# Two more source tiles in float32r, low parts by an accumulating transfer, and a ring of five logit buffers

## What is computed

```python
def gat_layer(x, W, att_src, att_dst, bias, src, dst, heads, out_ch, concat):
    n = x.shape[0]
    h = (x @ W.T).reshape(n, heads, out_ch)
    a_src = jnp.einsum('nhc,hc->nh', h, att_src)
    a_dst = jnp.einsum('nhc,hc->nh', h, att_dst)
    e = jax.nn.leaky_relu(a_src[src] + a_dst[dst], 0.2)
    m = jax.ops.segment_max(e, dst, num_segments=n)
    ex = jnp.exp(e - m[dst])
    denom = jax.ops.segment_sum(ex, dst, num_segments=n)
    alpha = ex / (denom[dst] + 1e-16)
    out = jax.ops.segment_sum(alpha[:, :, None] * h[src], dst, num_segments=n)
    return out.reshape(n, heads * out_ch) + bias        # concat
```

## Time and profile before

| | |
|---|---|
| median of three runs | 714.68 us |
| profiled execution, its own time | 713.25 us |
| its span | 711.4 us |
| TensorE (PE) busy | 701.1 us (99%) |
| TensorE's weight loads (PEld) | 657.9 us (92%) |
| VectorE (DVE) busy | 529.0 us (74%) |
| ScalarE (ACT) busy | 420.0 us (59%) |
| GpSimd (POOL) busy | 114.1 us (16%) |
| granted clock | 1.00 |

### The profile page before, as it was taken

One profiled execution on the slowest core, in us unless ns is written; L12 is line 12 of the kernel. 1 busy time (PEld: TensorE's weight loads), 2 busy tenths in 40 slices (PEclk: granted clock), 3 DMA queues, 4 the chain that ended last, 5 costly groups with the idle time before them and its releaser, 6 DMA issues.

```text
span 711.4 us, 13502 instructions
## 1 busy us (share of the span) xinstructions
PE 701.1 (99%) x4670; PEld 657.9 (92%) x4670; DVE 529.0 (74%) x878; ACT 420.0 (59%) x863; POOL 114.1 (16%) x95
## 2 busy tenths in 40 slices
PE   8899999999999999999999999999999999999997
PEld 6699999889899999999999999999999899999997
DVE  5999888698899999999999664445568752737232
ACT  4665584388688888888888754454443333522202
POOL 2559421000000000000000000000223331222202
PEclk9999999999999999999999999999999999999999
DMA  8727888645314131322310443201881734315102
GB/s 279 223 68 195 262 244 232 174 140 163 95 40 114 31 102 55 94 67 64 102 32 22 109 111 67 62 0 36 247 282 49 222 91 189 100 58 177 44 23 67
DMA packets 53362, 84.10 MB, mean 118 GB/s; under 512 B 15081, under 2 KB 36399, under 8 KB 53312
## 3 DMA queue, kind: packets, MB, share of 16 engines
q1 hardware_dynamic: 47628, 65.69, 32.6%
q10 hardware_dynamic: 4500, 13.82, 6.0%
q0 software_dynamic: 1184, 3.92, 1.9%
HBM read 68.09 MB, written 15.33 MB: 117 GB/s over the span
## 4 chain that ended last, share of the span: by engine, by line
PE 91%; DMA 4%; DVE 3%; issue 0%; POOL 0%; ACT 0%; ACTq 0%; SPq 0%; DVEq 0%
PE bank L1426 22%; PE bank L1571 13%; PE bank L1402 12%; PE bank L1498 12%; PE bank L1298 11%; PE bank L1675 4%; DMA w1n_sb<-in_W 3%; PE bank L1647 3%; PE bank L1213 3%; PE bank L1552 2%; PE bank L1701 1%; DVE x2f L2312 1%; PE bank L1215 1%; PE bank L1228 1%; PE bank L1732 1%; DVE fc_lo L2279 1%
## 5 line engine op out<-in xcount | busy, mean ns | idle before, releaser
L1426 PE MATMUL bank<-PT,h1s 125*128 125x250 f32 x730 | 161.0, 374 | 0.0
L1426 PEld LDWEIGHTS bank<-PT,h1s 125*128 125x128 f32 x730 | 135.3, 190 | 14.4
L2078 DVE SCALAR_TENSOR_TENSOR L<-asb,nadh 125x1250 f32<-125x1250 f32 x80 | 117.9, 1515 | 1.9 <-PE bank L1402 0.9
L2087 DVE CUSTOM_DVE_ANT_0 L<-L,LC 125x1250 f32<-125x1250 f32 x80 | 113.4, 1454 | 0.6 <-DMA LC<-log_count_scratch 0.4
L914 ACT ACTIVATE L<-L,nm 125x1250 f32<-125x1250 f32 x80 | 108.4, 1384 | 2.7 <-DVE nm L2087 1.9
L932 ACT COPY PT<-bank 125x500 f32<-125x500 f32 x165 | 87.4, 613 | 35.9 <-PE bank L1402 35.9
L1402 PE MATMUL bank<-ident,L 125*125 125x125 f32 x800 | 94.2, 273 | 0.0
L1402 PEld LDWEIGHTS bank<-ident,L 125*125 125x125 f32 x800 | 91.2, 189 | 0.9 <-issue 0.4
L1884 DVE TENSOR_TENSOR hotr<-iota,r 125x1500 f16<-125x1500 f16 x50 | 46.5, 931 | 7.8 <-PE bank L1215 4.2
L743 POOL MEMSET pick<- 128x90 f32 x1 | 0.2, 168 | 267.2 <-ACT hT L965 267.2
L1571 PE MATMUL bank<-h_hi,PT_hi 125*125 125x384 f32 x200 | 41.5, 350 | 0.0
(11 more groups left out here) (285 smaller groups left out, 1353.9 us busy)
## 6 DMA issues: line engine op xcount, KB each, us to landing
asb<-src_logit_rows SPq DMA_DIRECT2D x28, 312.5 KB, 3.9
atom_w<-in_atom_inT SPq DMA_DIRECT2D x5, 1152.0 KB, 12.5
atom_w<-in_atom_outT SPq DMA_DIRECT2D x5, 1152.0 KB, 9.4
log_count_scratch<-LCw SPq DMA_DIRECT2D x10, 546.9 KB
LC<-log_count_scratch SPq DMA_DIRECT2D x10, 546.9 KB
LCt<-log_count_scratch SPq DMA_DIRECT2D x10, 546.9 KB
h_scratch<-h1st ACTq DMA_DIRECT2D x10, 448.0 KB
rdT<-reciprocal_scratch SPq DMA_DIRECT2D x8, 500.0 KB, 4.6
```

The lines of the kernel that those rows point to most:

```text
L1426: mm = pe.matmul(sums, h1s[q][:, s, :], PT[p][:, s, :], start=(s == 0), stop=(plain and s == NT - 1))
L2078: dve.scalar_tensor_tensor(L[r][:, :], asb[q][0:NP, 1, :], nadh[q][:, t:t + 1], asb[q][0:NP, 0, :], ALU.add, ALU.max).then_inc(stt_done, 1)
L2087: dve.tensor_tensor_reduce(out=L[r][:, :], in0=L[r][:, :], in1=LC[:, t, :], scale=-1.0, scalar=-FLOOR, op0=ALU.add, op1=ALU.min, accum_out ...
```

## The change

Source tiles 0, 1 and 2 are split now, not tile 2 alone. Tile 0 is split as before, with VectorE's subtraction. For tiles 1 and 2 ScalarE writes a float32r high part and a raw copy with opposite signs, and the low parts are their sum, made by two transfers on POOL's queue: one copies the two raw tiles to PT_sum, the next adds the two high ones onto it. Signs are mended by features with the sign changed (`h1p_neg`). The features' low parts and the changed signs are POOL's now, three instructions a head. L has five buffers, and VectorE does in a step the second tile of its group and the first of the next (`blocks`). ScalarE does the first tile's exponential ahead of the evacuation, the second's behind it. To make room, the reciprocals' rows share one buffer, rdA lies where asb[1] does, and W2 is one transfer. asb is loaded in three pieces, and W2's products move to steps 3 and 4 of head 0.

```diff
-QUARTERS = 4
-PART = 2
+TURNED_BANKS = NG * NG * H
+PIECES = [0, 834, 1667, 2500]
+RING = 5
+PART = 0
...
+def blocks(k, first):
+
+    if first and k < 3:
+        return [(2 * k, 2 * k + 1)]
+    if first and k == 3:
+        return [(6,), (7, 8)]
+    if k == 0:
+        return [(0,), (1, 2)]
+    if k == 2 * NG - 1:
+        return [(2 * k + 1,)]
+    return [(2 * k + 1, 2 * k + 2)]
...
+            sp.wait_ge(wattp, 3)
+            sp.dma_start(w2_sb[:, :, 0:D], W2T.rearrange("(k p) n -> p k n", p=128)).then_inc(w2_in, 16)
...
+                if t < 2:
+                    sp.wait_ge(stt_done, NT * H)
...
+            def lower_by_sum(hh, kk):
+
+                n, p = 2 * NG * hh + kk, kk % 2
+                pool.wait_ge(tb_evac, NG * n + 2)
+                alone(pool)
+                pool.dma_start(PT_sum[p][:, :, :].bitcast(F32), PT[p][:, 1:3, :]).then_inc(raw_moved, 16)
+                pool.wait_ge(raw_moved, 16 * n + (16 - 16 * NG))
+                alone(pool)
+                pool.dma_start(PT_sum[p][:, :, :].bitcast(F32), PT_hi[p][:, 1:3, :].bitcast(F32), accum_op=ALU.add
+                               ).then_inc(lower_moved[p], 16)
+                if kk % NG == 0:
+                    q = kk // NG % 2
+                    pool.wait_ge(features_high, 2 * hh + kk // NG)
+                    alone(pool)
+                    pool.tensor_tensor(h1p_lo[q][:, 0:2, :], h1s[q][:, 0:2, :], h1p_hi[q][:, 0:2, :].bitcast(F32),
+                                       ALU.subtract)
+                    pool.tensor_tensor(h1p_lo[q][:, 2, :], h1p_hi[q][:, 2, :].bitcast(F32), h1s[q][:, 2, :],
+                                       ALU.subtract)
+                    pool.tensor_scalar(h1p_neg[q][:, :, :], h1p_hi[q][:, 1:3, :].bitcast(F32), -1.0, None, ALU.mult
+                                       ).then_inc(features_lower, 1)
+
+            for kk in range(NG, 2 * NG):
+                lower_by_sum(0, kk)
+            with pool.Fori(1, H // 2) as hh:
+                for kk in range(2 * NG):
+                    lower_by_sum(hh, kk)
...
                     if b == PART // 2 and not (first and k - lag < NG):
-                        act.copy(PT_hi[(k - lag) % 2][:, :], turned[0:NP, 0:GW])
-                        act.copy(PT[(k - lag) % 2][:, PART + 1, :], turned[0:NP, GW:2 * GW]).then_inc(tb_evac, 1)
+                        act.copy(PT_hi[(k - lag) % 2][:, 0:2, :],
+                                 turned[0:NP, 0:2 * GW].rearrange("p (s n) -> p s n", s=2))
+                        act.activation(PT[(k - lag) % 2][:, 1, :], turned[0:NP, GW:2 * GW], ACT.Copy, scale=-1.0
+                                       ).then_inc(tb_evac, 1)
+                    elif b == 1 and not (first and k - lag < NG):
+                        act.copy(PT[(k - lag) % 2][:, 2:4, :],
+                                 turned[0:NP, 0:2 * GW].rearrange("p (s n) -> p s n", s=2))
+                        act.activation(PT_hi[(k - lag) % 2][:, 2, :], turned[0:NP, 0:GW], ACT.Copy, scale=-1.0
+                                       ).then_inc(tb_evac, 1)
...
-                    if plain or s != PART:
-                        mm = pe.matmul(sums, h1s[q][:, s, :], PT[p][:, s, :], start=(s == 0), stop=(plain and s == NT - 1))
+                    if plain or s > 2:
+                        mm = pe.matmul(sums, h1s[q][:, s, :], PT[p][:, s, :], start=(s == (0 if plain else 3)), stop=(plain and s == NT - 1))
                 if not plain:
                     if g == 0:
                         pe.wait_ge(features_lower, h)
                     pe.wait_ge(lower_done, n + (1 - NG))
-                    pe.matmul(sums, h1p[q][:, 0, :], PT_hi[p][:, :], start=False, stop=False)
-                    pe.matmul(sums, h1p[q][:, 1, :], PT_hi[p][:, :], start=False, stop=False)
-                    mm = pe.matmul(sums, h1p[q][:, 0, :], PT_lo[p][:, :], start=False, stop=True)
+                    for s in range(3):
+                        high = h1p_neg[q][:, 1, :] if s == 2 else h1p_hi[q][:, s, :]
+                        pe.matmul(sums, high, PT_hi[p][:, s, :], start=False, stop=False)
+                        pe.matmul(sums, h1p_lo[q][:, s, :], PT_hi[p][:, s, :], start=False, stop=False)
+                    pe.matmul(sums, h1p_hi[q][:, 0, :], PT_lo[p][:, :], start=False, stop=False)
+                    pe.wait_ge(lower_moved[p], 16 * NG * hh + 16 * ((k - lag) // 2 - (NG // 2 - p)))
+                    pe.matmul(sums, h1p_neg[q][:, 0, :], PT_sum[p][:, 0, :], start=False, stop=False)
+                    mm = pe.matmul(sums, h1p_hi[q][:, 2, :], PT_sum[p][:, 1, :], start=False, stop=True)
...
-                if k == 6:
+                if k == 3:
...
+                for tiles in blocks(k, first):
+                    for s in tiles:
...
+                        if not (first and s < RING):
+                            dve.wait_ge(tb_full, NG * (2 * NG * hh + ((s - RING) // 2 + 1)))
```

More of the change, by code:

```diff
@@ L428, in gnn_ffn_kernel @@
         w1_hi_done, w1_lo_done, xT_lo_done = sem("w1_hi_done"), sem("w1_lo_done"), sem("xT_lo_done")
+        raw_moved, lower_moved = sem("raw_moved"), [sem(f"lower_moved{p}") for p in range(2)]
         features_high, features_lower, lower_done = sem("features_high"), sem("features_lower"), sem("lower_done")
@@ L905, in _, with exp @@
                     act.activation(early_exp[:, :], tiny[:, :], ACT.Exp)
-            def exp(hh, k, first=False, last=False):
+            def exp(hh, k, j, first=False, last=False):
                 if last:
@@ L949, in rows_out_of @@
                 act.wait_ge(rden_turned, m + 1)
-                to = rlast[:, ds(hh if k else hh + -1, 1), 0:NP] if (t0, t1) == (LATE, NT) else None
-                if to is None:
-                    to = rrow[t0:t1, ds(h, 1), 0:NP]
-                act.copy(to.rearrange("t a n -> t (a n)"), bank[4][0:t1 - t0, 0:NP]).then_inc(rden_rows, 1)
+                freed(act, rden_stored, 16 * m)
+                act.copy(rrow[0:t1 - t0, 0:NP], bank[4][0:t1 - t0, 0:NP]).then_inc(rden_rows, 1)
             def sums_out(hh, k, first=False, last=False):
@@ L1444, in turn_reciprocals @@
                     pe.wait_ge(rden_rows, m)
-                if first and k == NG + LATE // 2:
+                if first and k == NG:
                     pe.wait_ge(watt_done, 6)
@@ L2072, in logits @@
-                for j in range(2):
-                    r, t = (2 * k + j) % 4, 2 * g + j
-                    if not (first and k < 2):
-                        dve.wait_ge(tb_full, NG * n + -NG)
-                    elif k == 1:
-                        dve.wait_ge(lc_stored[0], TWO * NG)
-                    dve.scalar_tensor_tensor(L[r][:, :], asb[q][0:NP, 1, :], nadh[q][:, t:t + 1], asb[q][0:NP, 0, :],
-                                             ALU.add, ALU.max).then_inc(stt_done, 1)
-                reciprocals(hh, k, first=first)
```

167 lines of the change are left out of this document (87 added, 80 removed).

## The result

The changed kernel takes 732.62 us (median of four runs, 731.37 to 738.54) against 714.13 us for the kernel before (713.36 to 715.59, four runs): a ratio of 1.027, with a 95% interval of 1.025 to 1.030. It is **slower by 18.5 us**, where 710.5 was forecast, 4 us faster. The profiled execution has a span of 729.5 us against 711.4. One execution of a later run, e17_one_tile, took 998 us at a granted clock of 0.655 and is left out of its median.

A forecast was written before the change was run, and what follows sets the result against it. TensorE was taken as the bound, VectorE 3% behind. Terms -5.5 + 0.3 + 1.0 = -4.2 against the runs' median of 714.68 gave 710.5 us; range 708.0 to 733.0.

The forecast's parts named there:

- Step 1: TensorE in the head loops: two more split tiles save 0.156 us a step, -5.5 us over 35 steps.
- rival 3: TensorE's float32r products bound by weight loads in a run of nine: +10, 725 us; chance 0.03.
- Step 4: The two transfers a step on POOL's queue: 7.6 us for the pair within 10.0, hidden, cost 0.
- Rival 1: The pair of transfers comes too late, 125 rows on five engines: +20, 734.7 us; chance 0.24.
- Step 5: POOL's three operations a head exclude VectorE through a shared port: +1.0 us, between 0 and 14.
- rival 2: POOL's three operations hold VectorE and come late for TensorE at each head: 722.7 us; chance 0.17.
- Step 6: Head 0's moved W2 products 0, between -1 and +2; W2's one load 0; reciprocals' first loads 0.
- Steps 2 and 3: Head loop: VectorE stays 0.6 us a head behind the bound; ScalarE's added evacuation work costs +0.3 us, between 0 and 5.

The follow-up runs named there:

- e17_one_tile: Changed kernel with loads in pieces, early features, last two groups plain, reciprocals' transposition later, and only source tiles 0 and 1 split: 715.4 us, 1.002 of before.
- e3_neither: Changed kernel without the pair of transfers and without POOL's three operations a head (those terms left out or wrong): 713.29 us, 0.999 of the kernel before.
- e4_ring_only: Changed kernel with only source tile 0 split, its low part by VectorE, no transfers, nothing on POOL; ring and head 0's order stay: 715.37 us, 1.003 of before.
- e9_pieces: Changed kernel with loads of heads 2 to 7 in pieces, one a tile, and POOL's operations behind the raw transfer's issue: 727.29 us, 1.019 of before.
- e14_small_early_end: Changed kernel with 8-column loads in heads 2 to 7, features' parts made a step before the head, last two groups plain: 715.19 us, 1.002 of before.
- e6_early_features: Changed kernel with features' high part made a step before the head, POOL's operations behind that step's raw transfer issue: 727.21 us, 1.020 of before.
- e2_no_pool_ops: Changed kernel without POOL's three operations a head, products reading the features' high part instead; transfers stay: 727.52 us, 1.018 of before.

## Why the prediction was wrong

- **Step 1** (TensorE, -5.5) had the price of a step right. Steps without a wait are 0.14 to 0.16 shorter, starts 0.115 apart; rival 3 (weight loads) is excluded by them. The total was too large: between e3_neither and e4_ring_only it came to 3.7, since the steps with the reciprocals gave nothing.
- **Step 4 is the step that failed**: "the pair is 4.2 at the least, 7.6 by the median, 16.4 at the most; I take 7.6 ... and hidden: cost 0". The landings were good: 3.3 and 4.3 us by the median are 7.6. The slack was too large. An ordinary group shows it, the one that L1492 at 346.90 above belongs to:

```profile
337.45 0.57 POOL L767 DMA_DIRECT2D PT_sum<-PT  x1 [0.83 <-ACT PT L988]
341.48 0.86 POOL L770 DMA_DIRECT2D PT_sum<-PT_hi  x1 [3.46 <-DMA PT_sum<-PT]
```

The pair begins 2.8 us into its step (which starts at 334.60) and not 2.1. Between the raw landing and the adding issue 0.55 us pass, here and in every group, which the sum left out. The adding transfer lands 4.3 us after its issue, at 345.8, so 1.1 us are to spare and not 2.4. Over the 35 groups the pair takes 8.5 us by the median, in a budget of 9.5. The main fault was to price 35 pairs by one median. What costs is the slow tail, and it is not random. The last group of a head and the first of the next meet up to 1.5 MB of logit rows and features that SP sends just then, and the last three of all meet two loads of 1.0 MB of reciprocals. There one transfer takes up to 7.4 us, and a pair that TensorE waits for 9.7 to 12.3. The groups held it (the landing of 8.2 as the most, the logit rows of each head), and I read the 8.2 as an end of the range instead of asking which transfers it would be.
- **Rival 1** named the place (the last two products wait for the transfer) and, by luck, nearly the time, 734.7. Its mechanism was another: five engines for 125 rows. That is excluded, since raw transfers landed in 3.3 us by the median, where it gave 5.7 each, and since the pair costs nothing when it is alone. It also expected all 35 steps to lengthen by 0.57; in fact 18 of the steps 6 to 39 gained 0.1 to 0.2, and eight lost 0.8 to 2.9, 13.3 us together.
- **What no step priced is the clock.** A wait of TensorE of 2.1 us was followed by a stretch of 6 us at 0.80, which nearly doubled what the wait cost. Before had no such wait, so its trace could not show it.
- **Step 5 and rival 2** (POOL's operations: +1.0, or up to 14): 5.1 us with the pair, 3.0 early and without loads, 0 without the pair. The mechanism of rival 2, an operation held by VectorE's instructions, is in the rows of e9_pieces (5.3 us for the three, where the prediction had 5.9, but 2.3 by themselves and not 1.5, and less than a whole instruction each). VectorE is held as well: the addition ahead of the reciprocals (125x6) took 1.57 us at 264.27 in the changed kernel, beside those operations, and 0.16 in e14_small_early_end, where they are not beside it. That POOL and VectorE hold each other up agrees with the rule of the Trainium skill (SBUF — State Buffer, "SBUF: two separate sides") that the prediction drew on. Since e6_early_features gets 5.4 us back with the operations still made, they cost mostly as one more thing in POOL's queue behind a late transfer, which the prediction added up but only at a raw landing of 3.8.
- **Step 6** (head 0: "0, between -1 and +2") came out at 2 in e4_ring_only, the end of its range, and between 1.2 and 3.8 in the other profiles with its order, for the reason that it weighed (VectorE waits for the logit rows) and one that it did not see: the fourth buffer now waits for a store of LC. That the loads of the reciprocals "were issued only at 393.57" and cost 0 was wrong: they run beside the pairs of the last groups. In step 38 the change lost 2.75 us and behind the start of step 39 another 2.9; TensorE's waits there:

```profile
413.79 0.58 PE L1492 MATMUL bank<-PT_sum,h1p_neg 125*128 125x250 f32 x1 [2.34 <-DMA PT_sum<-PT_hi]
...
428.26 0.38 PE L1492 MATMUL bank<-PT_sum,h1p_neg 125*128 125x250 f32 x1 [2.27 <-DMA PT_sum<-PT_hi]
```

- **Steps 2 and 3** (VectorE, ScalarE) held in the main: both kept up in clean steps, with ScalarE 115.08 us busy of 128 against 110.72 in the earlier trace rows, but not in the steps with the reciprocals (9, 19 and 29), which e3_neither has 0.1 to 0.4 us longer than before.

Open: what head 0's wait for the store of LC costs by itself, where the 5.1 us between the changed kernel and e2_no_pool_ops lie, and what the reciprocals' loads would cost if they were cut or held back (no run changes them). A version with the raw transfer left out (ScalarE writing straight to where the adding transfer adds) was not run.

## What to carry to other kernels

Price a transfer that must land within a budget by its slowest meeting, not by its median: list which other loads are in flight at each of its occurrences, and look for the place in the loop where they bunch. Count what lies between the two as well: here 0.55 us from a landing to the next issue were part of the 1.3 us of slack that the sum had too much. Large loads beside it can be cut into pieces, one for each unit of work. With all the bytes kept, that, the operations' early place and a plain end took TensorE's waits for the pair from 9.0 to 0.4 us. An engine's queue in front of such a transfer is part of its latency, so small work goes where nothing is behind it that someone waits for. And a gain of 0.15 us a step is gone with one wait of 2 us that costs 4.0, when the clock falls after it, in nearly thirty steps.

## What the runs showed of the hardware

- A transfer of 244 KB from SBUF to SBUF on POOL's queue, 125 rows of 2000 bytes, lands 2.8 us after issue at the least and 3.3 by the median; the same with an addition 3.9 and 4.3. With next to nothing beside them the medians were 2.8 and 3.9. The first took up to 7.3 beside some 1.5 MB of loads, the second up to 7.2 beside 1.0 MB.
- From the landing of such a transfer to the start of the next issue that waits for it on POOL's queue 0.55 us passed (0.55 to 0.60 in every group of the changed kernel).
- After TensorE had been idle for 2.1 us in a loop at full clock, the granted clock was 0.92 and then 0.80 in stretches of 6 us (part of the time at 1.2 GHz and part at 2.4), and float32r products started 0.21 to 0.28 apart instead of 0.115.
- A POOL operation of 128 columns took 0.53 us (264.91) and 1.67 us (225.07, beside back-to-back VectorE instructions). A VectorE instruction of 125x6 took 0.16 us alone and 1.57 beside POOL's operations.
